# A graph layer and a mixture of experts: head in rows, picks with the table as weights, end stages in pieces, and a bound on how far GpSimd runs ahead

## What is computed

```python
x = x + gnn(layernorm(x), src, dst)
x = x + experts(layernorm(x))

def gnn(x):
    h = batch_norm(x @ w1.T + b1, g1, bt1)          # statistics over the 6250 nodes
    m = segment_max(h[src] - h[dst], dst)           # 0 where a node has no edge
    hg = gelu(batch_norm(concat(h, m) @ wg.T + bg, gg, btg))
    return batch_norm(hg @ w2.T + b2, g2, bt2) + x

def experts(x):                                     # 8 experts, softmax weights per node
    w = softmax(x @ Wr + br)
    return sum over e of w[e] * (relu(bn(relu(bn(x @ W1[e] + b1)) @ W2[e] + b2)) @ Wo[e] + bo)
```

## Time and profile before

| what | value |
|---|---|
| median of 3 executions | 3184.01 us |
| profiled execution, its own time | 3195.85 us |
| its span, first to last instruction | 3194.1 us |
| mean granted TensorE clock | 0.955 |
| PE busy | 2845.5 us, 89% |
| DVE busy | 2206.5 us, 69% |
| ACT busy | 1920.1 us, 60% |
| POOL busy | 1550.7 us, 49% |
| moved by transfers | 606.33 MB, mean 190 GB/s |

### The profile page before, as it was taken

One profiled execution on the slowest core, in us unless ns is written; L12 is line 12 of the kernel. 1 busy time (PEld: TensorE's weight loads), 2 busy tenths in 40 slices (PEclk: granted clock), 3 DMA queues, 4 the chain that ended last, 5 costly groups with the idle time before them and its releaser, 6 DMA issues. The chain is left out here.

```text
span 3194.1 us, 52861 instructions
## 1 busy us (share of the span) xinstructions
PE 2845.5 (89%) x21180; PEld 2692.2 (84%) x21213; DVE 2206.5 (69%) x4110; ACT 1920.1 (60%) x2617; POOL 1550.7 (49%) x1530
## 2 busy tenths in 40 slices
PE   5389999999999999999999994697699999999998
PEld 4289999898989899998989893587598998989988
DVE  7499877787878788787778783387555555555544
ACT  3377767776767767676767661316365555555554
POOL 3377777777777777777777775541000000000000
PEclk8699999999999999999999996898899999999999
DMA  7867667676766777666767666720323233233231
GB/s 237 300 220 254 236 238 241 231 245 225 251 227 237 240 244 237 238 236 229 255 223 249 231 238 211 285 63 1 114 100 122 90 128 113 97 119 111 99 114 67
DMA packets 188187, 606.33 MB, mean 190 GB/s; under 512 B 32368, under 2 KB 83654, under 8 KB 180772
## 3 DMA queue, kind: packets, MB, share of 16 engines
q1 hardware_dynamic: 116180, 406.35, 34.3%
q0 software_dynamic: 71760, 196.60, 20.5%
HBM read 340.13 MB, written 262.69 MB: 189 GB/s over the span
## 5 line engine op out<-in xcount | busy, mean ns | idle before, releaser
L665 POOL DMA_INDIRECT ring<-ztab,src_i x1436 | 1450.7, 1010 | 485.4 <-issue 415.9
L985 PE MATMUL ps<-zh,oh 128*128 128x256 f32 x6272 | 1569.9, 290 | 101.0 <-DVE oh L838 94.4
L986 PE MATMUL ps<-zl,oh 128*128 128x256 f32 x6272 | 1541.7, 286 | 0.0
L985 PEld LDWEIGHTS ps<-zh,oh 128*128 128x128 f32 x6272 | 1221.7, 195 | 115.9 <-DVE oh L838 106.2
L986 PEld LDWEIGHTS ps<-zl,oh 128*128 128x128 f32 x6272 | 1223.5, 195 | 0.0
L832 DVE SCALAR_TENSOR_TENSOR ring<-ring,pen 128x256 f32<-128x256 f32 x1564 | 749.8, 479 | 384.0 <-DMA ring<-ztab,src_i 368.4
L680 ACT ACTIVATE oh<-ids,nodeneg 128x512 fp32r<-128x512 f32 x896 | 639.0, 718 | 465.3 <-PE ps L986 465.2
L685 ACT ACTIVATE oh<-oh,ones 128x512 fp32r<-128x512 f32 x896 | 613.1, 708 | 0.0
L838 DVE TENSOR_SCALAR oh<-ps,nodef 128x512 fp32r<-128x512 f32 x672 | 500.6, 745 | 11.2 <-PE ps L986 10.9
L1447 ACT ACTIVATE av<-ps,vecs 128x896 f32<-128x896 f32 x224 | 246.2, 1099 | 348.8 <-PE ps L194 348.8
L1559 DVE TENSOR_TENSOR h2l<-av,h2h 128x896 fp32r<-128x896 f32 x112 | 122.3, 1093 | 212.9 <-ACT h2h L1449 212.9
(11 more groups left out here) (254 smaller groups left out, 3329.9 us busy)
## 6 DMA issues: line engine op xcount, KB each, us to landing
runs<-ring SPq DMA_DIRECT2D x136, 896.0 KB, 4.4
fw<-wsp SPq DMA_DIRECT2D x56, 1536.0 KB, 6.5
runs<-ring SPq DMA_DIRECT2D x102, 768.0 KB, 4.3
ring<-ztab,src_i POOLq DMA_INDIRECT x1436
zs<-zs_d SPq DMA_DIRECT2D x14, 896.0 KB, 11.7
ids<-srcT_d SPq DMA_DIRECT2D x32, 256.0 KB, 5.5
zT_d<-zc SPq DMA_DIRECT2D x7, 896.0 KB
res_d<-x_all SPq DMA_DIRECT2D x7, 896.0 KB, 6.7
```

Source lines behind the costliest of these rows:

```text
L665: pool.indirect_dma_start(ring[:, k, :], None, ztab, bass.IndirectOffsetOnAxis(ap=src_i[:, STEPS * i + k:STEPS * i + k + 1], axis=0)).then ...
L985: pe.matmul(o, hot, block_h, start=False, stop=False, skip_group_check=True)
L986: r = pe.matmul(o, hot, block_l, start=False, stop=False, skip_group_check=True)
```

## The change

- **Head in rows.** The sign goes into the weights. The transposed rows' high and low parts become the weights of the matmul and w1 the moving operand, so z comes out in rows and needs no turning back; the bias enters by one more matmul per tile (`one2`, `bb`). Normalizing moves from VectorE to ScalarE and is done in place. z stays in SBUF and is stored once, to `runs`, from which the gathers now read. The residual store holds the normalized rows alone (chunk 0 excepted); the input is added later.
- **Statistics** of the table are taken at the start of the next block from transposes into PSUM, before the first chain step.
- **Picks.** The table is the weights, 128 features at a time, and the one-hots are the moving operand, 512 columns: four matmuls per block. The result is transposed, so ScalarE copies it out (`picks_out`), TensorE turns it back after group 1 of the next round, and `result` stands after group 2.
- **Rounds 16 to 31** no longer split the transposed table; the sums beside rounds 32 and 33 take it from SBUF by transposes (`columns`).
- **The hold.** GpSimd waits, at every fourth gather of a group, until the chain has passed the gather's step minus 21.
- **End stages.** Turning, splitting, evacuating and statistics go in pieces of 512 and 384 columns; all gathered maxima have their own place; GELU's table is loaded early; GELU's first half is split block by block.
- **Expert layers.** The input x is added to `y` by an accumulating transfer that GpSimd issues, for chunks 1 to 6.

```diff
+LEAD = 21
@@ head: SyncE
-                def store(c, last):
-                    wait(sp, s_zc, 2 * c + 2)
-                    sp.dma_start(zT_d[:, :, bass.ds(c * CW, CW)], zc[:]).then_inc(s_zts, 16)
-                    wait(sp, s_xr, c + 1)
-                    sp.dma_start(rows(res_d, c, last), x_all[:, bass.ds(c * TPC, TPC), :]).then_inc(s_store, 16)
-                    wait(sp, s_tab, c + 2)
-                    sp.dma_start(rows(ztab, c, last), tabc[:]).then_inc(s_store, 16)
-                    if not last:
-                        sp.dma_start(rows(runs, c, last), tabc[:]).then_inc(s_store, 16)
...
-                    wait(sp, s_store, 48 * c + (32 if last else 48))
-                    sp.sem_inc(s_tfree, 1)
+                for c in range(1, NCH - 1):
+                    sp.dma_start(x_all[:, c * TPC:(c + 1) * TPC, :], rows(io["x"], c, False)).then_inc(s_x[c], 16)
...
+                for c in range(NCH):
+                    sp.wait_ge(s_h0, c + 1)
...
+                    sp.dma_start(rows(res_d, c, False), x_all[:, c * TPC:(c + 1) * TPC, :]).then_inc(s_store, 16)
+                    sp.wait_ge(s_z, c + 1)
+                    if c < NCH - 1:
+                        sp.dma_start(rows(runs, c, False), z_all(c)).then_inc(s_store, 16)
@@ head: ScalarE, TensorE
+                for c in range(NCH):
+                    z_out(c)
+                    if c + 2 < NCH:
+                        hi(c + 2)
+                    if c + 3 < NCH:
+                        apply(c + 3)
+                    if c + 4 < NCH:
+                        root(c + 4)
...
+                def mm(c):
+                    pe.wait_ge(s_lo, c + 1)
+                    if c:
+                        pe.wait_ge(s_z, c)
                     for t in range(TPC):
+                        o, cols = banks(4, 4)[:, t * C:(t + 1) * C], slice(t * P, (t + 1) * P)
+                        pe.matmul(o, one2[:], bb[:], start=True, stop=False)
+                        r = three(pe, o, [((h0h[c % 2][:, k, cols], h0l[c % 2][:, k, cols]), (w1h[:, k, :], w1l[:, k, :])) for k in range(KC)],
+                                  False, True)
+                    r.then_inc(s_Z, 1)
@@ rounds: GpSimd
                         if i:
                             pool.wait_ge(s_st[g], 16 * i)
-                            pool.wait_ge(s_ch, STEPS * (i if g == NG - 1 else i - 1) + GO[g + 1] % STEPS + 1)
                         for k in range(GO[g], GO[g] + by_pool(i, g)):
-                            pool.indirect_dma_start(ring[:, k, :], None, ztab,
+                            if (k - GO[g]) % 4 == 0 and STEPS * i + k > LEAD:
+                                pool.wait_ge(s_ch, STEPS * i + k - LEAD)
+                            pool.indirect_dma_start(ring[:, k, :], None, runs[0:N, :],
@@ rounds: VectorE, before the first step
-                bn_vectors(dve, KC, dv("tmp")[:, 0:2], vec("bt1"), dv("a1"), dv("c1"), s_bnv, s_bsd, 1)
+                for c in range(NCH):
+                    z_stats(c, c == NCH - 1)
+                dve.drain()
+                bn_moments(dve, KC, s_bnv)
@@ rounds: TensorE
-                            for s in range(NPE):
-                                o = ps[:, two + s // 2, s % 2 * C:(s % 2 + 1) * C]
-                                hot = oh[:, v, s * P:(s + 1) * P]
-                                pe.matmul(o, hot, block_h, start=False, stop=False, skip_group_check=True)
-                                r = pe.matmul(o, hot, block_l, start=False, stop=False, skip_group_check=True)
+                            for k in range(KC):
+                                cols = slice(k * P, (k + 1) * P)
+                                pe.matmul(ps[:, two + k, :], z_hi(g)[:, v, cols], oh[:, v, :], start=g == 0 and v == 0, stop=False,
+                                          skip_group_check=True)
+                                r = pe.matmul(ps[:, two + k, :], z_lo(g)[:, v, cols], oh[:, v, :], start=False,
+                                              stop=False, skip_group_check=True)
                             r.then_inc(s_ohf, 1)
+                        if g == 1 and i:
+                            turn_back(i - 1)
@@ end of the rounds: SyncE
-                for j in range(3):
-                    half(j)
-                for g in range(NG):
-                    store(PG, g)
-                    half(3 + g)
...
+                for i in (PG, PG + 1):
+                    for g in range(NG):
+                        store(i, g)
@@ end of the rounds: TensorE
+                for n in range(NPIECE):
...
                     for m in range(GM):
+                        sums(n, m)
+                        if m % 2 and n + 2 < NPIECE:
+                            columns(n + 2, m // 2)
@@ end stages: VectorE, last chunk; ScalarE
+                def finish(c, m):
+
+                    for b, (a, w) in enumerate(PIECES):
+                        dve.wait_ge(s_G, 2 * (GM * c + m) + b + 1)
+                        gs = gT[:, c, m, a:a + w]
+                        r = dve.tensor_tensor(gs, ps[:, 4 + 2 * (m % 2) + b, 0:w], gs, ALU.add)
...
+                        dve.bn_stats(bnst[:, m, 2 * c + b, :], gT[:, c, m, a:a + LASTP[b][1]])
+                    dve.drain()
+                    dve.bn_aggr(bmv[:, m, :], bnst[:, m, :, :].rearrange("p a b -> p (a b)"))
...
+                act.activation(fine[:, 495:496], dv("eps"), ACT.Gelu_apprx_tanh)
@@ expert layers: GpSimd
+                for c in range(1, NCH):
+                    pool.wait_ge(s_res[c % 3], 16 * (c // 3 + 1))
+                    if c < NCH - 1:
+                        pool.dma_start(y[:, c % 3, :, :], rows(io["x"], c, False), accum_op=ALU.add).then_inc(s_rx[c % 3], 16)
```

More of the change, by code:

```diff
@@ L533, in _ @@
[L533 to L543 removed]
+                norm(2)
+                measure(3)
+                low(1)
@@ L554, in _ @@
+                for c in range(NCH - 2):
+                    if c + 3 < NCH:
+                        norm(c + 3)
+                    if c + 4 < NCH:
+                        measure(c + 4)
+                    low(c + 2)
+                    if c == 0:
+                        penalties()
+                    elif c < 4:
+                        digits(c - 1)
             @block.tensor
@@ new lines, in sums @@
+                def sums(n, m):
+                    _, _, w = piece_of(n)
+                    if n:
+                        pe.wait_ge(s_aev, GM * (n - 1) + m + 1)
+                    if m == 0:
+                        pe.wait_ge(s_tev, KC * n + KC)
+                    cols = slice(m * P, (m + 1) * P)
+                    three(pe, ps[:, 4 + m, 0:w],
+                          [((wah[:, k, cols], wal[:, k, cols]), (zs[n % 3][:, 0, k, 0:w], zs[n % 3][:, 1, k, 0:w])) for k in range(KC)],
+                          True, True).then_inc(s_A, 1)
@@ L1004, in _ @@
+                columns(0, 0)
+                columns(0, 1)
                 pe.wait_ge(s_wa, 32)
@@ L1165, in step @@
+                low(0, 0)
+                low(0, 1)
+                for c in range(NCH - 1):
                     g_out(c, 0)
+                    dve.drain()
+                    stats(c, 0)
                     g_out(c, 1)
+                    dve.drain()
+                    stats(c, 1)
+                    low(c + 1, 0)
                     g_out(c, 2)
-                    if not last:
-                        low(c + 1, 1 - par)
+                    low(c + 1, 1)
+                    dve.drain()
+                    stats(c, 2)
@@ L1170, in step @@
                     g_out(c, 3)
                     dve.drain()
-                    for m in range(GM):
-                        stats(c, m, last)
-                low(0, 0)
-                paired(dve, step)
+                    stats(c, 3)
+                for m in range(GM):
+                    finish(NCH - 1, m)
                 dve.drain()
-                bn_vectors(dve, GM, vec("gg"), vec("btg"), dv("ag"), dv("cg"), s_bnv, s_bsd, 2)
+                dve.sem_inc(s_bnv, 1)
+                bn_affine(dve, GM, vec("gg"), vec("btg"), dv("ag"), dv("cg"), s_bsd, 2)
@@ new lines, in sums @@
+                def sums(c, m):
+                    pe.wait_ge(s_gev, GM * c + m + 1)
+                    cols = slice(m * P, (m + 1) * P)
+                    for b, (a, w) in enumerate(PIECES):
+                        if m == 0:
+                            pe.wait_ge(s_ml, 2 * c + b + 1)
+                        three(pe, ps[:, 4 + 2 * (m % 2) + b, 0:w],
+                              [((wbh[:, k, cols], wbl[:, k, cols]), (mh[:, c % 2, k, a:a + w], ml[:, c % 2, k, a:a + w])) for k in range(KC)],
+                              True, True).then_inc(s_G, 1)
@@ L1202, in _ @@
                 turn(0)
                 pe.wait_ge(s_wbl, 1)
-                paired(pe, step)
+                for c in range(NCH):
+                    sums(c, 0)
+                    sums(c, 1)
+                    if c < NCH - 1:
+                        turn(c + 1)
```

(2 more changed lines are left out.)

784 lines of the change are left out of this document (385 added, 399 removed).

## The result

The kernel after takes 3106.01 us (median of 4, 3101.80 to 3109.14), the kernel before 3184.86 in the same comparison: 0.9752 of it, 95% interval 0.9735 to 0.9769. The forecast was 3109. The profiled execution of after has a span of 3104.8 us and an own time of 3106.59, so it lies 0.6 above its median, where that of before lay 11.0 above this one (11.8 above the median that the prediction used).

The account below looks back on a forecast made before the run. GpSimd's gather pace and start were taken to bound the rounds, with TensorE hidden under them. Terms -36 + 2 - 7 - 18 - 16 = -75 gave 3121 for the profiled execution, 3109 for the median; range 3086 to 3148.

Parts of the forecast that it names:

- head: Head in rows, loop 7.7 us a chunk: first gather at about 93 instead of 130, minus 36 us (minus 45 to plus 2).
- hold, picks, splits, pace: Rounds: hold plus 2 us, picks nothing, no splitting in rounds 16 to 31 minus 7, gathers' pace not in the sum.
- last two rounds: GpSimd's 18.3 us wait for a store goes, as loads between the stores go: minus 18 us (-18 to +9).
- end stages: Neighbour stage and GELU piece by piece: 5 + 2 + 5 + 1 + 3, minus 16 us (-5 to -20).
- expert layers: Input added by an accumulating transfer on GpSimd's otherwise empty queue, with a chunk's time to land: nothing.
- about 3 us: Head's start: second chunk's normalization and transposes ahead of the first matmul move it from 24.1 to 27.
- Statistics, hold, picks: Chain starts 25 us after first gather, hidden; hold costs 2 (0 to 11); picks 47.4 us a round under 54.9, nothing.
- the sixteen splits: Rounds 16 to 31: sixteen VectorE low parts go, each stretching gathers by 0.44 us: minus 7 us (0 to 12).
- The three us of cover: Last two rounds: TensorE's sums end 108 us after round 31's last step, the chain 111, so sums stay hidden.
- Half clock in the head: Rival: head's matmuls stay at 1.2 GHz, loop 13.6 us, first gather at 132, time 3147; chance 0.07.
- TensorE the bound: Rival, rounds: mean clock below 0.86 makes TensorE the bound; at 0.80 plus 139, so 3248; chance 0.06.
- the low part's price: Rounds: one VectorE low part stretches the gathers beside it by 0.44 us; the full lock rule would give 0.95.

Follow-up runs that it names:

- head_v3: Kernel after with both small rows and first two input chunks loaded first, other loads waiting, last chunk stored in two parts: 3623.7 us, slower chip kind, 0.901 of before.
- low_out: Kernel after without the low halves of the picks, 98 of 196 pick matmuls a round left out: 3100.5 us, 0.9730 of before.
- halves: Kernel after with each pick matmul of 512 columns split into two of 256: 3107.6 us, 0.9747 of before.
- before_again: Kernel before, unchanged, profiled a second time, on a chip of the slower kind: 4064.9 us.
- end_whole: Kernel after with the last chunk's statistics behind its four sums and GELU's first half taken whole: 3620.4 us on a chip of the slower kind.
- after_again: Kernel after, unchanged, on a chip where the kernel before takes 4021 us: 3608.2 us, 0.900 of before.
- split3_b: Kernel after with three more VectorE instructions shaped like the low part in each of 32 pick rounds: 3579.9 us, beside 3608.2 of after.
- head_best: Kernel after with the second input chunk loaded ahead of the bias row and the last chunk stored in two parts: 3103.4 us, 0.9738 of before.

## Why the prediction was right

The mechanism held on the chip of the comparison: GpSimd's pace and its start set the rounds, and the gain came from the places that were named. That this chip was an ordinary one is luck, because on a starved chip the rounds have another bound. Profile against profile, by the steps of the sum:

| step | forecast | measured | between |
|---|---|---|---|
| head | -36 | -30.3 | start and first gather: 129.8, 99.5 |
| hold, picks, splits, pace | -5 | -20.0 | first gather and round 32's first: 1773.7, 1753.7 |
| last two rounds | -18 | -19.5 | there and the chain's end: 140.6, 121.1 |
| end stages | -16 | -19.3 | there and the first expert product: 235.7, 216.4 |
| expert layers | 0 | -0.2 | there and the end: 914.3, 914.1 |
| sum | -75 | -89.3 | spans 3194.1, 3104.8 |

The medians differ by 78.9. The forecast of 3109 is so close because two misses cancel: the sum is 14 short, and the 11.8 us that the profiled execution of before lay above its median were carried over, where after's lies 0.6 above. Why that execution was long is open.

*Head.* The loop is 7.85 us a chunk (35.04 to 90.0 for seven) against 7.7, the store 91.8 to 99.5 as thought. What failed is "about 3 us" for the second chunk's normalization: its transfer was counted in bytes for the head as a whole (74 us hidden in 93) and not at the one place where the first product waits for it, 6.96 us. head_v3 and low_out show that as the cause. A slip beside it: the lower bound of 85 for the first gather is 27 + 2 + 54 + 3 = 86.

*Statistics, hold, picks.* The chain starts 25.3 us behind the first gather, forecast 25. The hold costs 0, not 2; the 25 unasked gathers are as worked out. Picks: nothing, shown by halves.

*Splits and pace.* -7 for the sixteen splits is too much. From round 16 to 31 GpSimd gains 11.1 us (879.6 to 868.5), in the twelve rounds before them, where the split is left as it was, 6.2 (659.4 to 653.2): 8.3 for sixteen, so about 3 belong to the splits. Another 10 lie in all rounds: 7 ns in the median of 1436 gathers (960 to 953). The prediction bounded the gathers' pace by 3 ns and put it at nothing in the sum. What sets those 7 ns is open; before_again shows that they are no chance of one execution. The remaining 7 of the 20 us are not traced.

*Last two rounds.* The chain ends 110.0 us after round 31's last step, forecast 111; the sums at 109.9, forecast 108. The three us of cover are 0.1.

*End stages.* The steady part gives 6.4 (87.5 to 81.1 between first and last product) where 5 were counted. The start, from the first gather of neighbours to the first product, gives 4.6 (16.6 to 12.0) instead of 2, and the fix ahead of it 1.0. The idling before GELU's products falls by 7.7 where 9 were counted. There the 5 for the statistics was the wrong reading: VectorE has the same work in either order, end_whole gives 1.6 for it, 2 for GELU by blocks where 3 were counted, and leaves 1.2 for the table where 1 was; the others of the 7.7 are not divided.

*Expert layers.* Nothing, as forecast. The accumulating transfer, of which the prediction had no row, lands in 13.2 us for 896 KB, twice the 6.7 and far within a chunk's time.

*Rivals.* Half clock in the head: no, 0.12 us a matmul from 35.2 on, granted clock 0.97. The trace of before had spoken against it already. Within its first group, after the idling, the distance falls from the 0.43 us of the earlier trace rows to 0.23:

```profile
28.78 0.40 PE L192 MATMUL ps<-h0h,w1h 128*128 128x512 f32 x1
29.01 0.39 PE L193 MATMUL ps<-h0l,w1h 128*128 128x512 f32 x1
```

TensorE the bound: not on the ordinary chip (0.96, GpSimd without a wait). On the starved chips GpSimd waits for the chain in every round, and not because of the clock alone (0.88 in the rounds of after_again, above the 0.86 of the rival), but with TensorE's work reported late; the prediction had no such case. For the low part's price, the rows give 0.56 us in split3_b and 0.44 in before, of the 0.95 that it lasts. The Trainium skill (SBUF — State Buffer, section Who interferes with whom) calls contention on the port pair that VectorE and GpSimd share an exclusive lock; "for the whole instruction" stands there of VectorE's 2-port modes, and of two SBUF inputs that they contend. Read in full for those too, as the prediction weighed it, that gives 0.95, and the gathers show about half. VectorE's 4.01 us in head_best agree with a lock to the end, beside a GpSimd addition and not a gather.

## What to carry to other kernels

Work out a transfer's landing at the instruction that waits for it first, not as bytes under a long stage. Moving an engine's work earlier gives little (1.6 us of the 5 forecast here) while that same engine still has to finish all of it before the next stage. And a hold that is worth nothing on one chip can be worth a tenth of the rounds on another (75 to 67 us): ask which resource each edit relieves, even where the profile at hand has plenty of it.

## What the hardware showed unexpectedly

The same kernel takes 3185 us on some chips and 4016 to 4048 on others, and the change is worth 2.5% on the first and 10% on the second (0.900 [0.894, 0.905]). On the latter, while GpSimd's gathers run, an engine that waits for TensorE goes on up to 10 us (with the hold of 21) or 18 us (with 40) behind the end that the profile shows for TensorE's matmuls, and TensorE at times runs its instructions one or two at a time, 0.7 to 1.4 us apart. This ends when GpSimd stands, and the head and the expert layers are not slowed. What distinguishes the chips, and what is late, no row shows. The clock granted in the rounds is 0.81 there instead of 0.97 in before and 0.88 instead of 0.96 in after.
